# A new order of all engines ahead of the first attention step, in a kernel for attention and top-2 experts

## What is computed

```python
h = layernorm(x)
q, k, v = h @ Wq.T + bq, h @ Wk.T + bk, h @ Wv.T + bv
x = x + softmax(q @ k.T / 16 + 2 * adj) @ v          # adj is 1354 x 1354
h = layernorm(x)
s = h @ router_w + router_b                           # 8 experts, the best 2 of softmax(s)
e = (h @ w1 + b1);  g = silu(e @ wg + bg) * (e @ wv + bvv)
x = x + sum over the chosen 2 of p * (g @ w2 + b2)    # w1 256x512, wg/wv 512x512, w2 512x256
```

## Time and profile before

| | us |
|---|---|
| three executions | 483.78, 486.17, 487.23 (median 486.17) |
| profiled execution | 483.35 |
| its span, first to last instruction | 481.6 |
| TensorE / VectorE / GpSimd / ScalarE busy in the span | 401.1 / 317.1 / 245.5 / 181.9 |
| first matmul (Wv turned) | starts at 11.06 |
| first value row product | starts at 18.80 |
| `scores_of(0)` | starts at 57.09 |
| third group of probabilities of tile 0 turned, in step 1 | starts at 93.98 |
| step 2 of the attention | starts at 105.36 |
| step 3 | starts at 120.87 |

### The profile page before, as it was taken

How to read it: one execution, slowest core, us unless ns; L and a number is a source line. 1 busy time by engine, 2 the same in 40 slices (tenths; PEclk the granted TensorE clock), 3 DMA queues, 4 the chain that set the end, 5 groups by cost and what they waited for, 6 DMA issues and landing times.

```text
span 481.6 us, 8057 instructions
## 1 busy us (share of the span) xinstructions
PE 401.1 (83%) x2279; PEld 342.9 (71%) x2279; DVE 317.1 (66%) x747; ACT 181.9 (38%) x321; POOL 245.5 (51%) x255
## 2 busy tenths in 40 slices
PE   0957775899999999999997793969998999999920
PEld 0846654699889988998886572658777788888810
DVE  4544545577778988898877870476565576767671
ACT  1245443454555455545544341612222233323200
POOL 2113745575448655865686546270887460005482
PEclk9996879999999999999999796979999999999985
DMA  8650026537565567576548599123665641113253
GB/s 238 233 208 12 0 103 205 168 114 242 172 197 171 194 192 228 162 238 189 177 122 306 173 279 309 58 99 80 249 239 189 230 154 56 56 55 114 83 159 103
DMA packets 44860, 78.93 MB, mean 164 GB/s; under 512 B 5278, under 2 KB 25186, under 8 KB 43796
## 3 DMA queue, kind: packets, MB, share of 16 engines
q1 hardware_dynamic: 33844, 65.27, 41.0%
q10 hardware_dynamic: 8352, 7.61, 5.0%
q0 software_dynamic: 2624, 5.56, 3.9%
HBM read 56.13 MB, written 22.29 MB: 163 GB/s over the span
## 4 chain that ended last, share of the span: by engine, by line
PE 65%; DMA 11%; DVE 8%; issue 4%; ACT 4%; POOL 2%; SPq 2%; DVEq 1%; ACTq 1%; POOLq 0%
PE ps L902 28%; PE ps L1175 18%; PE ps L1071 6%; DMA expert_out<-ysum 3%; PE ps L1073 3%; DVE acc L1303 3%; PE ps L1024 2%; POOL picked L644 2%; DMA xblk<-expert_rows 2%; PE ps L1207 2%; DMA first_row<-in_L_ffn_bv 1%; DMA expert_rows<-zeros 1%; PE ps L1152 1%; DMA picked<-expert_out,ypos_i 1%; PE ps L945 1%
## 5 line engine op out<-in xcount | busy, mean ns | idle before, releaser
L555 POOL TENSOR_TENSOR lo<-raw,hi 128x512 fp32r<-128x512 f32 x60 | 75.7, 1291 | 66.9 <-DVE acc L1303 66.9
L1175 PE MATMUL ps<-weights,bT_hi 128*128 x232 | 74.0, 400 | 0.0
L902 PE MATMUL ps<-hi,w1T_lo 128*128 128x512 f32 x128 | 55.7, 435 | 4.5 <-DVE w1T_lo L1226 3.1
L1175 PE MATMUL ps<-weights,bT_lo 128*128 x116 | 50.0, 431 | 7.9 <-issue 5.2
L902 PE MATMUL ps<-hi,w1T_hi 128*128 128x512 f32 x128 | 52.9, 413 | 0.0
L902 PE MATMUL ps<-lo,w1T_hi 128*128 128x512 f32 x128 | 52.5, 410 | 0.0
L644 POOL DMA_INDIRECT picked<-expert_out,ypos_i x22 | 24.5, 1112 | 55.0 <-DMA expert_out<-ysum 48.9
L1175 PEld LDWEIGHTS ps<-weights,bT_hi 128*128 128x128 f32 x232 | 44.9, 194 | 7.8
L1071 PE MATMUL ps<-v,pT_hi 128*128 128x256 f32 (+3 forms) x242 | 44.7, 286 | 0.0
L1175 PE MATMUL ps<-weights,gT_hi 128*128 x232 | 42.6, 281 | 0.0
L1576 DVE TENSOR_TENSOR ps<-ps,bias 128x512 f32<-128x512 f32 x29 | 20.3, 699 | 30.9 <-PE ps L1175 20.2
(11 more groups left out here) (204 smaller groups left out, 974.5 us busy)
## 6 DMA issues: line engine op xcount, KB each, us to landing
raw<-in_L_ffn_wg SPq DMA_DIRECT2D x8, 1024.0 KB, 6.2
raw<-in_L_ffn_wv SPq DMA_DIRECT2D x8, 1024.0 KB, 7.5
products<-ring SPq DMA_DIRECT2D x28, 256.0 KB, 4.1
landed<-products SPq DMA_DIRECT2D x7, 1024.0 KB, 7.3
adj_sb<-in_adj SPq DMA_DIRECT2D x10, 677.0 KB
bias<-biases SPq DMA_DIRECT2D x8, 640.0 KB, 5.4
w1raw<-in_L_ffn_w SPq DMA_DIRECT2D x8, 512.0 KB, 4.9
landed<-in_L_ffn_w SPq DMA_DIRECT2D x8, 512.0 KB, 4.2
```

The lines of the kernel that those rows point to most:

```text
L555: G.tensor_tensor(lo[j % RAWS][:, k, :], raw[j % RAWS][:, k, :], r32(hi[j % HIS][:, k, :]), ALU.subtract).then_inc(m_lo, 1)
L902: last = nc.tensor.matmul(o, a, b, start=n == 0, stop=n == len(m) - 1)
L1175: last = nc.tensor.matmul(o, stationary[i][:, k, :], part(e, ats[j] + k * width, width), start=n == 0, stop=n == len(m) - 1)
```

## The change

Everything up to the first attention step gets a new order. The steps, the experts and the end are untouched, except for the waits named here.

- Wv, Wk, Wq, bk and bq are loaded from ScalarE's queue; bk lies as a column of Wk, so that Wq.T·[Wk | bk] gives wqk and its bias in one product, ahead of everything else.
- The inverse square roots are done by groups: group 0 on VectorE (14 serial small instructions), groups 1 and 2 on GpSimd (14 each). A seventh value, -mean·y, lets ScalarE normalise (`x_rows`, an activation with scale and bias), into what is later `xn2_all`.
- The value rows are split straight from PSUM: hi on ScalarE, lo on VectorE. bv is added to x instead (the rows of a softmax sum to one), by 11 additions on GpSimd (`add_bv`) after `matrix_lo(3)` and ahead of step 1.
- TensorE does queries, turned w1 and the products of matrix 0 between the value tiles; the first four products go to banks 4, 5, 3, 5.
- `gather_bias` comes in blocks of two or four. The wait for the stored products moves from `pT_part(0)` to `normalise2(0)`.

```diff
+                return (SPARE, COMB, 3, COMB)[i]      # bank_of(i), i < 4
 # SP
-            for n, w in enumerate((Wq, Wk, Wv)):
-                sp.dma_start(wraw[:, n, :, :], w.rearrange("(k p) d -> p k d", p=P)).then_inc(w_in, 16)
             sp.dma_start(b1rows[:, :], b1.rearrange("e (k p) -> (e k) p", p=P)).then_inc(b1_in, 16)
+            load_w1(0)
+            load_raw(0)
+            load_first_row(0)
             load_small(bv_row ...); load_small(rb ...); load_small(rw ...)
             load_raw(1)
             load_adj(0)
+            load_small(biases[:, B_AT[2]:B_AT[2] + D], b2)
             load_w1(1)
             load_raw(2)
             load_raw(3)
             load_first_row(1)
+            store_product(0)
             load_first_row(2)
+            store_product(1)
+            load_raw(4)
+            store_bias_row(0)
             sp.wait_ge(logits_done, 1)
             load_adj(1)
 # GpSimd
-            for t in range(TILES):
-                v_rest(t)
-                if 6 <= t < 6 + KH:
-                    ...
-                    chunk_lo(0, t - 6)
+            for g in range(1, len(GROUPS)):
+                finish_factors(pool.wait_ge, G, g, pool)
+            pool.wait_ge(m_hi, 1)
+            for k in range(KH):
+                pool.wait_ge(acc_done, k + 1)
+                chunk_lo(0, k)
             sum_lo(0)
             for j in (1, 2, 3):
                 matrix_lo(j)
                 sum_lo(j)
+            pool.wait_ge(small_in, n_small[0])
+            for t in range(TILES):
+                add_bv(t)                 # x1 += bv_row, waits xn_done
 # ScalarE
+                act.dma_start(wv_raw ...); act.dma_start(wk_raw ...); act.dma_start(wq_raw ...)
+                act.dma_start(wk_raw[:, :, D], bk ...); act.dma_start(bqk[:, 0, :], bq ...)
+            act.wait_ge(wvT_mm, 1)
+            copy(wvT[0][:, :, 0:D], by_k(ps[:, 5, :], KD)).then_inc(wvT_hi, 1)
+            x_rows(0)
+            x_rows(1)
+            act.wait_ge(small_done, 1)
+            copy(wvT[0][:, :, D:VW], bk_turned[:, :, :]).then_inc(wvT_hi, 1)
+            x_hi(0)
+            x_rows(2)
+            x_hi(1)
+            act.wait_ge(wqk_mm, 1)
+            copy(wqk[0][:, :, :], ps[:, 4:7:2, 0:D]).then_inc(wqk_hi, 1)
+            x_rows(3)
+            for t in range(TILES):
+                if t + 2 < TILES: x_hi(t + 2)
+                v_part(t)
+                if t + 4 < TILES: x_rows(t + 4)      # waits factors_done of its group
+                if t == 2: w1_hi(0, 0, 4); w1_hi(0, 1, 5)
+                if t == 3: matrix_hi(0); keep_q(0); ...; q_part(0)
+                if t == 6: matrix_hi(1); keep_product(0)
+                if t == 7: sum_hi(0); keep_q(1)
+                if t == 8: keep_product(1)
+                if t == 9: sum_hi(1)
+            keep_q(2)
...
+            matrix_hi(2)
+            keep_bias_row(0, MIX)
             probabilities(0)
+            keep_product(2)
             q_part(1)
+            w1_hi(1, 0, SPARE)
             sum_hi(2)
             keep_bias_row(1, MIX)
             matrix_hi(3)
+            keep_product(3)
+            w1_hi(1, 1, MISC)
             sum_hi(3)
 # TensorE
+            (Wv turned; then Wq.T . [Wk | bk], 4 matmuls of 258 columns, wqk_mm)
+            transpose_x(0)
+            transpose_x(1)
+            turn_biases()                 # 2 + 4 matmuls of one column, waits bqk_mult
+            for t in range(TILES):
+                if t + 2 < TILES: transpose_x(t + 2)
+                value_rows(t)             # waits xT_lo t+1, v_lo t-1
+                if t == 0: (b1 turned)
+                if t == 2: pe.wait_ge(wqk_lo, 1); turn_w1(0, 0, 4); turn_w1(0, 1, 5)
+                if t == 3: queries(0)
+                if t == 6: multiply(0, 0)
+                if t == 7: queries(1)
+                if t == 8: multiply(0, 1)
+            queries(2)
             scores_of(0)
-            multiply(0, 0); sum_bias(0); turn_w1(1, 0); multiply(0, 1); sum_bias(1)
-            multiply(1, 0); turn_w1(1, 1); multiply(1, 1)
+            sum_bias(0, MIX)
+            multiply(1, 0)
+            turn_w1(1, 0, SPARE)
+            turn_w1(1, 1, MISC)
+            multiply(1, 1)
+            sum_bias(1, MIX)
 # VectorE
+            statistics(0)
+            rough_factors(0)
+            finish_factors(dve.wait_ge, V, 0, dve)
+            (wvT lo); dve.wait_ge(wqk_mm, 1); (bk_turned, bqk_each)
+            statistics(1)
+            rough_factors(1)
+            ...
+            for t in range(TILES):
+                if t + 2 < TILES: x_rest(t + 2)
+                v_rows(t)                 # row_add, then v lo from PSUM
+                if t == 0: statistics(2); rough_factors(2)
+                if t == 1: (wqk lo); (b1T)
+                if t == 2: w1_rest(0, 0, 4); w1_rest(0, 1, 5)
+                if t == 3: gather_bias(0); q_rest(0)
+                if t == 6: gather_bias(1, (0, 1)); first_rest(0)
+                if t == 7: gather_bias(1, (2, 3))
+                if t == 8: first_rest(1)
+            gather_bias(2)
             logits(0)
+            first_rest(2)
+            w1_rest(1, 0, SPARE)
             q_rest(1)
+            first_rest(3)
+            w1_rest(1, 1, MISC)
             gather_bias(3)
```

More of the change, by code:

```diff
@@ L343, in newton, with factors_of, finish_factors, step @@
                 engine.tensor_scalar(y, tmp, 1.5, y, ALU.add, ALU.mult).then_inc(newton2, 1)
+        def factors_of(g):
+            t0, n = GROUPS[g]
+            return [mv[:, t0:t0 + n, 0], mv[:, t0:t0 + n, 1]] + [rs[:, i, t0:t0 + n] for i in range(4)]
+        def finish_factors(wait_ge, engine, g, queue):
+            mean, _, var, y, tmp, shift = factors_of(g)
+            count = 14 * g
+            def step(ins):
+                nonlocal count
+                count += 1
+                ins.then_inc(newton1, 1)
+                wait_ge(newton1, count)
+            wait_ge(rough1, 2 * g + 2)
+            for _ in range(3):
+                step(engine.tensor_tensor(tmp, y, y, ALU.mult))
+                step(engine.tensor_tensor(tmp, tmp, var, ALU.mult))
+                step(engine.tensor_scalar(tmp, tmp, -0.5, 1.5, ALU.mult, ALU.add))
+                step(engine.tensor_tensor(y, tmp, y, ALU.mult))
+            step(engine.tensor_tensor(tmp, mean, y, ALU.mult))
+            step(engine.tensor_scalar(shift, tmp, -1.0, None, ALU.mult))
+            queue.sem_inc(factors_done)
         PASSES = ((1, 0), (0, 1), (0, 0))
@@ L693, in keep_product, with x_rows @@
                     copy(ring[:, i % 2, :], ps[:, bank_of(i), :]).then_inc(prod_done, 1)
-            act.wait_ge(wvT_mm, 1)
-            copy(wvT[0][:, :, 0:D], by_k(ps[:, 5, :], KD)).then_inc(wvT_hi, 1)
+            with nc.allow_non_contiguous_dma("bk as a column"):
+                act.dma_start(wv_raw[:, :, :], Wv.rearrange("(k p) d -> p k d", p=P)).then_inc(wv_in, 16)
+                act.dma_start(wk_raw[:, :, 0:D], Wk.rearrange("(k p) d -> p k d", p=P)).then_inc(wqk_in, 16)
+                act.dma_start(wq_raw[:, :, :], Wq.rearrange("(k p) d -> p k d", p=P)).then_inc(wqk_in, 16)
+                act.dma_start(wk_raw[:, :, D], bk.rearrange("(k p) -> p k", p=P)).then_inc(wqk_in, 16)
+                act.dma_start(bqk[:, 0, :], bq.rearrange("(k p) -> p k", p=P)).then_inc(bq_in, 16)
+            def x_rows(t):
+                w = width(t)
+                g = [i for i, (t0, n) in enumerate(GROUPS) if t0 <= t < t0 + n][0]
+                act.wait_ge(factors_done, g + 1)
+                nc.scalar.activation(xn2_all[:w, t, :], x1[:w, t, :], ACT.Identity,
+                                     bias=rs[:w, 3, t:t + 1], scale=rs[:w, 1, t:t + 1]).then_inc(xn_done, 1)
             def x_hi(t):
@@ L1231, in rough_rsqrt @@
                 return V.tensor_scalar(y.bitcast(I32), var.bitcast(I32), -0.5, MAGIC, ALU.mult, ALU.add)
-            def rsqrt(var, half, y, tmp, done, count):
-                def step(ins):
-                    nonlocal count
-                    count = count + 1
-                    ins.then_inc(done, 1)
-                    wait(dve, done, count)
-                step(V.tensor_scalar(half, var, EPS, None, ALU.add))
-                step(rough_rsqrt(y, half))
-                step(V.tensor_scalar(half, half, -0.5, None, ALU.mult))
-                for _ in range(3):
-                    step(V.tensor_tensor(tmp, y, y, ALU.mult))
-                    step(V.tensor_tensor(tmp, tmp, half, ALU.mult))
-                    step(V.scalar_tensor_tensor(y, tmp, 1.5, y, ALU.add, ALU.mult))
             V.memset(mv[:, :, :], 1.0).then_inc(mv_done, 1)
@@ L1372, in normalise2 @@
                 dve.wait_ge(newton2, NEWTON2 * (t + 1))
+                if t == 0:
+                    for r in range(2):
+                        dve.wait_ge(prod_out[r], 64)
                 V.tensor_scalar(xn2_all[:n, t, :], x1[:n, t, :], mv2[:n, 0:1], ln2[:n, 1:2],
```

344 lines of the change are left out of this document (162 added, 182 removed).

## The result

The changed kernel took 470.01 us (median of four runs, 469.35 to 471.68) against 486.7 for the kernel before (four runs): ratio 0.966, 95% interval 0.958 to 0.973, 16.7 us faster. Forecast were 466 and a gain of 20, range 457 to 479.

The account below looks back on a forecast made before the run. The prelude was taken as bound by a chain of hand-overs, no engine full before 94 us. Step 2 29.0 us earlier, less 4 (clock), 4 (GpSimd) and 1 (contention), gives 20: 486.2 - 20 = 466 us, range 457 to 479.

Parts of the forecast that it names:

- The start: Loads to first value product: last weight there at 7.5, first value product at 15.2 instead of 18.80.
- late weights: Rival at the start: Wq, Wk and bk land only at 11, 4.7 us less gained, 471 us; chance 0.14.
- Tiles 0 to 10: First value product to queries' end: 23.8 us of TensorE work plus 5.65 of charges, ending at 44.6.
- The named waits: Charges within the tiles: group 1's factors 1.15, wqk lo 1.1, tile 8's rows 0.5, matrix 0's lo 1.2.
- (c): Contention of GpSimd with VectorE, sums beside matrix lo or bv: 1 us off the gain, ends 0 and 5.
- To the third group: Queries' end to step 1's third group: turned at 65.0 instead of 93.98, step 2 at 76.4, 29.0 earlier.
- (a): TensorE's clock in the prelude, half rate after idle stretches: 4 us off the gain, ends 0 and 8.8.
- the walk: Engine orders followed from start to step 2, with half rate charged 1.7 at two value tiles: 29.0 us earlier.
- (b): GpSimd late behind step 1 through bv's additions, TensorE waiting in step 2: 4 us off, ends 0 and 7.8.
- The signs: Milestones to show the forecast right, like step 2 at 76 to 81, or wrong, like first value product near 20.
- Slower: Rival in the steps: GpSimd never catches up and holds TensorE each step, 497 us at 4 a step; chance 0.04.
- Head of line: Rival in the prelude: big blocks and a late 2 KB row cost 6 us, clock 4.8 more, 477; chance 0.18.

Follow-up runs that it names:

- w1_x_held_only: Changed kernel with bv added once per step, group 1's statistics earlier, ScalarE's matrix 3 copy later, x groups 1 and 2 held until Wv landed: 460.85 us.
- y1: Changed kernel with bk loaded ahead of Wk and Wq, and SP's w1, matrices and all behind them held until these landed: 471.35 us, ratio 0.967.
- x1_bv_spread: Changed kernel with the eleven additions of bv spread, one in each step, instead of all ahead of matrix 4: 464.16 us, ratio 0.956.
- y2: Changed kernel with ScalarE's copy of matrix 3 behind product 3 and w1 hi instead of ahead of them: 469.07 us, ratio 0.963.
- z1: Changed kernel with bv spread, statistics earlier, matrix 3 later, bk and bq first on SP's queue, x groups 1 and 2 behind Wv: 466.63 us.
- w0: Changed kernel with bv spread, statistics earlier, matrix 3 later, bk and bq first on SP's queue, no x held: 466.3 us, ratio 0.957.

## Why the prediction was right, and where its terms were off

**The start.** Forecast for the last weight 7.5, measured 10.73: the 3.2 us is the rival of late weights in part, and the step that failed is "I take 7.5 for the last to be there". It took bk's 4.8 us from the earlier trace rows, where bk stood in one queue with x and the weights; issued at 2.46 on ScalarE's queue, beside x on SP's, it took 8.2. w1_x_held_only shows the cause: with x of groups 1 and 2, and all behind them, held, 7.02 is reached, while y1, which held only what stands behind x, gained nothing. The value product was only 2.3 late, since transposes and one-column matmuls ran faster than at the prices taken.

**Tiles 0 to 10.** From the first value product to the end of the queries 29.4 were forecast and 31.5 came. The named waits were there in their places: rows of tile 4 1.75 (forecast 1.15), wqk lo 0.6 (1.1), tile 8 2.14 (0.5), matrix 0's lo 0.52 (1.2). The third is the one mis-sized, and it waited not for tile 8's rows on ScalarE but for VectorE's x lo of tile 6: VectorE's three sums and the queries' lo ran beside GpSimd's chunks, 3.24 instead of 2.33 and 1.48 instead of 0.41:

```profile
28.41 3.24 DVE L1353 SCALAR_TENSOR_TENSOR acc<-raw,b1T,acc 128x512 f32<-128x512 f32 x3
31.57 1.48 DVE L1294 TENSOR_TENSOR qs_lo<-qT,qs_hi 128x256 fp32r<-128x256 f32 x1
```

So (c), taken as 1, cost 2 there alone, and the exclusive lock of the Trainium skill (SBUF — State Buffer, SBUF: two separate sides) is what these rows look like: an instruction of 0.41 with two operands in SBUF took 1.1 us more beside GpSimd. That the ports do it was not tested alone. The up to 2.8 us that the prediction gave for matrix 4's sums by this section of the Trainium skill came at those sums too, but beside GpSimd's lo of matrix 3 and not beside the additions of bv: the three after the first took 5.06 instead of 2.33. TensorE had no wait from there to 93.5, so it cost nothing:

```profile
70.67 5.06 DVE L1353 SCALAR_TENSOR_TENSOR acc<-raw,b1T,acc 128x512 f32<-128x512 f32 x3
```

**To the third group.** 20.4 us from the scores' start were forecast and 20.8 came. TensorE's product 2 was forecast 60.1 to 62.9, inside the chain of the others. It waited 2.96 us and then ran at half rate, 64.54 to 69.80, and so was itself the last:

```profile
64.54 0.77 PE L951 MATMUL ps<-hi,w1T_lo 128*128 128x512 f32 x1 [2.96 <-DVE w1T_lo L1294]
65.11 0.63 PE L951 MATMUL ps<-lo,w1T_hi 128*128 128x512 f32 x1
65.53 0.63 PE L951 MATMUL ps<-hi,w1T_hi 128*128 128x512 f32 x1
```

**(a) The clock.** Taken as 4 us, beside the 1.7 that the walk had charged for tiles 0 and 1. Those ran at full rate (value matmuls 0.12 apart from 17.73 on). Half rate stood from 22.8 to 26.2 and from 63.8 to 70.6 in the prelude; both times it began while TensorE stood idle. The first stretch, as in the earlier trace rows:

```profile
23.00:26.00 3.00, 2.70 (x13) 2.70 (x14) 1.88 (x7) 1.89 (x5) 1.44 (x8) 0.50 0.00 0
```

In it the turned w1 took 1.76 us instead of 0.79, and tile 3 1.49 instead of 0.96; product 2 took 5.26 instead of 2.77: 4.0 in all, where walk and (a) together had 5.7. For the prelude that is right in size, though the first part stood elsewhere than charged.

**(b) GpSimd behind step 1.** The lateness was right: forecast 9.7 us after the start of step 2, measured 92.4 - 81.95 = 10.4. The two waits were right too, third group and w1 lo, forecast "Together 4", measured 2.86 + 1.20:

```profile
96.41 0.50 PE L1141 MATMUL ps<-v,pT_hi 128*128 128x256 f32 x2 [2.86 <-DVE pT_lo L1294]
99.17 0.79 PE L951 MATMUL ps<-hi,w1T_lo 128*128 128x512 f32 x1 [1.20 <-DVE w1T_lo L1294]
99.77 0.63 PE L951 MATMUL ps<-lo,w1T_hi 128*128 128x512 f32 x1
```

But step 2 was 7.0 us longer, not 4, and this is the term that was mis-sized most: behind the two waits the 12 matmuls took 5.49 instead of 2.77, at 1.2 instead of 2.4 GHz. Waits of 4.1 us cost 7. The prediction had the clock as a term of the prelude, and none for what the waits of step 2 would do to it. x1_bv_spread takes all of it back at once, 6.4 us at step 3. In the sum, 29.0 became 23.3 by step 2 with clock and contention in it (forecast 24), and 7.0 went where 4 were charged: 16.3 instead of 20. That 23.3 lies so near to 24 is in part luck: the weights' 2.3 stood in no term of the sum, and all else that came off was 3.4 where clock and contention had 5.

**The signs.** The first value product (17.5, said near 15), the queries' end (49.0, near 45), the third group (69.8, 65 to 69) and step 2 (81.95, 76 to 81) all came late, by 1 to 4 us; the scores before 50 and the one long step with its two waits came as said. ScalarE's wait for the factors of group 1 was 1.95, just below the 2 that was to count against the forecast. The sign "steps above 16 us from step 4 on" was badly drawn: they take 16.1 in the kernel before as well (first line) as in the changed one, and the 15.5 of a step held for step 2 alone, ahead of the first routing.

```profile
136.86:152.99 16.13, 16.13 (x102) 14.35 (x101) 13.70 (x35) 8.37 (x15) 8.94 (x11) 1.00 0.63 199
136.87:153.00 16.13, 16.13 (x103) 14.36 (x101) 13.75 (x36) 8.36 (x15) 10.70 (x16) 1.00 0.59 183
```

**The rivals.** GpSimd did catch up: step 3 took 16.1 us against 16.0 before, so "Slower" did not come near. The 470.0 lies nearer to the 471 of late weights than to 466, but the weights account for 2.3 us of it, and the slow matmuls of step 2 for 2.7. Head of line: the row of 2 KB caused no wait; VectorE did stand for product 0's hi, 1.8 us, with tile 9's x lo behind it. With the clock rule of the Trainium skill (TensorE: Matmul & The Clock Gate, What's actually happening) the trace agrees in direction: from 17 to 94 us the denser order was granted 0.93 against 0.84. It did not keep the full rate, which fell again at a wait of 3 us.

## What to carry to other kernels

When a serial prelude is reordered, walk every engine's queue past the end of the changed part: work that was taken off a full engine and set ahead of another engine's next duty comes back as a wait one stage later, and a wait of TensorE costs more than itself, as the matmuls behind it may run at half rate. Put such work where the engine has room in each step, one piece at a time. A wait that is only shortened can give back more than itself: in y2, behind 1.16 us instead of 2.96, the product ran at full rate. Of loads at the start, hold back what is needed later rather than move the urgent one to another queue, and don't set loads of many 4-byte pieces ahead of a large one.

## What was not expected of the hardware

- Two loads of 1 KB, each a column of 4-byte pieces, ahead of x on SP's queue made x's first 512 KB land at 8.6 to 8.7 us instead of 5.3 to 5.5 (z1, w0 against w1, x1 and the changed kernel).
- Holding 0.85 MB of x, and all behind it on SP's queue, until Wv had landed brought Wq's landing from 7.4 to 4.8 us after its issue, and bk's from 8.6 to 4.6.
- 12 matmuls after idle times of 2.96 us, and of 2.86 and 1.20 us close together, took 5.26 and 5.29 us from start to start instead of 2.77; in x1_bv_spread, with no wait in step 2, the clock stayed at 1.00 there, and in y2, behind 1.16 us, the 12 took 2.8.
- The clock fell at different places in executions of the same order: in y2, whose edit lies further on, it was 0.50 from 36 to 38, in the changed kernel 1.00. That moved the first scores by 1.0 us, as much as some of the edits are worth; why it fell there is not shown.
